# Expert results stored by route tile, rows gathered by token in the next stage: one core of a two-layer transformer kernel

## The reference, cut to what matters

```python
hn2 = _layernorm(x, ln2_g, ln2_b).reshape(-1, h)          # 4096 tokens
logits = hn2 @ gate_w + gate_b
idx = jnp.argmax(logits, axis=-1)                          # one of 8 experts per token
mid = jax.nn.relu(jnp.einsum('th,ehf->etf', hn2, w1) + b1[:, None, :])
y = jnp.einsum('etf,efh->eth', mid, w2) + b2[:, None, :]
moe = y[idx, jnp.arange(hn2.shape[0])]                     # only the chosen expert's row
return x + moe.reshape(b, s, h)
```

## Time and profile before

| what | us |
|---|---|
| median of the 3 runs shown | 1943.62 (1942.78 to 1947.55) |
| the profiled execution, its own time | 1934.06 |
| its span, first to last instruction | 1932.2 |
| mean granted PE clock over the span | 0.929 of full speed |
| PE busy / DVE / ACT / POOL in the span | 1711.6 / 1568.5 / 1332.0 / 1119.9 |

### The profile page before, as it was taken

One profiled execution on the slowest core, in us unless ns is written; L12 is line 12 of the kernel. 1 busy time (PEld: TensorE's weight loads), 2 busy tenths in 40 slices (PEclk: granted clock), 3 DMA queues, 4 the chain that ended last, 5 costly groups with the idle time before them and its releaser, 6 DMA issues. The chain is left out here.

```text
span 1932.2 us, 48344 instructions
## 1 busy us (share of the span) xinstructions
PE 1711.6 (89%) x18519; PEld 749.4 (39%) x18519; DVE 1568.5 (81%) x2890; ACT 1332.0 (69%) x2816; POOL 1119.9 (58%) x740
## 2 busy tenths in 40 slices
PE   6528756999999984969999999999999999999997
PEld 3328742233333354954432333333333333333334
DVE  7853466999999934648879999999999999999963
ACT  4502234688999852637866778887888888888885
POOL 8813553000010027431137889999999999989995
PEclk9769878799999975979988999999999999999998
DMA  1230027111111133248993332323232323233311
GB/s 49 33 56 4 2 75 272 36 45 47 45 45 47 33 108 108 74 116 292 405 365 87 82 81 76 87 69 87 70 89 68 89 71 86 75 81 80 77 29 44
DMA packets 194393, 178.08 MB, mean 92 GB/s; under 512 B 58740, under 2 KB 155156, under 8 KB 194084
## 3 DMA queue, kind: packets, MB, share of 16 engines
q1 hardware_dynamic: 185764, 167.93, 30.2%
q0 software_dynamic: 2944, 7.10, 1.2%
q10 hardware_dynamic: 5504, 0.73, 0.2%
HBM read 99.08 MB, written 75.26 MB: 90 GB/s over the span
## 5 line engine op out<-in xcount | busy, mean ns | idle before, releaser
L1038 ACT ACTIVATE probs_l<-exp_l 128x512 f32<-128x512 f32 x1024 | 575.6, 595 | 177.4 <-PE exp_l L1077 171.5
L976 DVE TENSOR_REDUCE maxima_l<-max_l 128x1 f32<-128x512 f32 x1024 | 640.5, 683 | 33.2 <-PE max_l L1122 33.1
L952 POOL TENSOR_TENSOR part_sums_l<-probs_l 128x1024 f32<-128x1024 f32 x256 | 604.0, 2359 | 91.5 <-ACT probs_l L1038 78.7
L1077 PE MATMUL exp_l<-q_stack_l,k_stack_l 100*128 100x512 f16 x1024 | 392.8, 385 | 3.4 <-ACT probs_l L1038 3.1
L1122 PE MATMUL max_l<-k_stack_l,q_stack_l 96*128 96x512 f16 x1024 | 387.2, 389 | 4.8 <-DVE pv_bank_l L968 3.6
L1361 DVE TENSOR_REDUCE maxima_l<-max_l 128x1 f32<-128x512 f32 x512 | 316.1, 683 | 13.3 <-PE max_l L1465 13.1
L1415 ACT ACTIVATE probs_l<-exp_l 128x512 f32<-128x512 f32 x512 | 278.8, 605 | 42.3 <-PE exp_l L1478 37.7
L1093 PE MATMUL pv_bank_l<-probs_l,v_ring_l 128*32 128x512 f32 x2048 | 273.7, 606 | 0.5 <-ACT probs_l L1038 0.5
L1077 PEld LDWEIGHTS exp_l<-q_stack_l,k_stack_l 100*128 100x128 f16 x1024 | 98.5, 97 | 395.0 <-ACT probs_l L1038 364.6
L1297 POOL TENSOR_SCALAR rstd_l<-squares_l 128x4 f32<-128x4 f32 x7 | 1.6, 234 | 339.9 <-ACT junk_l L1400 339.9
L958 POOL TENSOR_TENSOR part_sums_l<-part_sums_l 128x512 f32<-128x512 f32 x128 | 163.2, 1275 | 10.1
(11 more groups left out here) (305 smaller groups left out, 2422.6 us busy)
## 6 DMA issues: line engine op xcount, KB each, us to landing
scratch_qk_l<-parts_g SPq DMA_DIRECT2D x128, 256.0 KB, 9.2
q_stack_l<-scratch_qk_l SPq DMA_DIRECT2D x192, 128.0 KB
k_stack_l<-scratch_qk_l SPq DMA_DIRECT2D x192, 128.0 KB
scratch_v_l<-v_g SPq DMA_DIRECT2D x16, 1024.0 KB, 10.8
v_ring_l<-scratch_v_l SPq DMA_DIRECT2D x64, 256.0 KB, 3.4
scratch_stack_l<-parts_c SPq DMA_DIRECT2D x16, 384.0 KB, 3.5
q_stack_l<-scratch_stack_l SPq DMA_DIRECT2D x64, 96.0 KB, 2.2
k_stack_l<-scratch_stack_l SPq DMA_DIRECT2D x64, 96.0 KB, 2.3
```

What stands on the lines that cost most here:

```text
L952: pool.tensor_tensor(part_sums[:, i, h, :, :], probs[:, i, h, 0:2, :], probs[:, i, h, 2:4, :], ALU.add).then_inc(pair_sum.sem, 1)
L976: dve.reduce_max(maxima[:, s % 2, at % NT, at // NT:at // NT + 1], max_bank(n, at)[:, :], AX).then_inc(max_taken.sem, 1)
L1038: act.activation(probs[:, i, at // NT, at % NT, :], exp_ps[at % 2][:, :], ACT.Exp, scale=a.scale).then_inc(prob_tile.sem, 1)
L1077: pe.matmul(exp_ps[at % 2][:, :], ks[0:SHIFT_ROW + HG, slot, h, k * P:(k + 1) * P], qs[0:SHIFT_ROW + HG, slot, h, :], start=True, stop=Tru ...
```

## The change

The second scatter goes. Each route's result is stored by SP with a plain DMA to `by_route`, a DRAM tensor with one 128-row tile per route, ten routes behind the loads in SP's own stream. DVE works out for each token the row of `by_route` that holds its result (`g.dest`), behind the table. In the preparation POOL gathers each of the 32 tiles with an indirect DMA into `g.y`. The token number leaves the rows, so a row has 128 words.

```diff
-ROW = D + 1
-    r.rows, r.zeros = sb("rows", [P, T, ROW]), sb("zeros", [P, 2 * E_, ROW])
+    r.rows, r.zeros = sb("rows", [P, T, D]), sb("zeros", [P, 2 * E_, D])
-            did(pool.iota(r.rows[:, :, D:ROW]...))
-                did(pool.iota(r.zeros[:, :, D:ROW]...))
+STORE_LAG = 10
 # moe, SP
-            for i in range(ROUTES):
-                if i >= SLOTS:
-                    sp.wait_ge(y_out[i % DEPTH], 16 * ((i - SLOTS) // DEPTH + 1))
-                    sp.wait_ge(oneT_ps.sem, oneT_ps.made(i - SLOTS, 0))
-                at = sp.value_load(table[0:1, 0, i:i + 1], ...)
-                sp.dma_start(got[:, i % SLOTS, :], scratch.sorted[bass.ds(at, P), :]).then_inc(got_in[i % SLOTS], 16)
-            for s in range(DEPTH):
-                sp.wait_ge(y_out[s], 16 * (ROUTES // DEPTH))
-            for b in range(B):
-                sp.dma_start(g.y[:, b * NT:(b + 1) * NT, :], scratch.by_token[b * N:(b + 1) * N, :]...).then_inc(g.back_in[b], 16)
+            for i in range(ROUTES + STORE_LAG):
+                if i < ROUTES:
+                    if i >= SLOTS:
+                        sp.wait_ge(oneT_ps.sem, oneT_ps.made(i - SLOTS, 0))
+                    at = sp.value_load(table[0:1, 0, i:i + 1], ...)
+                    sp.dma_start(got[:, i % SLOTS, :], scratch.sorted[bass.ds(at, P), :]).then_inc(got_in[i % SLOTS], 16)
+                if i >= STORE_LAG:
+                    n = i - STORE_LAG
+                    sp.wait_ge(y_sb.sem, y_sb.made(n, 0))
+                    sp.dma_start(g.by_route[n * P:(n + 1) * P, :], y[:, n % DEPTH, :]).then_inc(y_out[n % DEPTH], 16)
 # moe, POOL
-            for i in range(ROUTES):
-                pool.wait_ge(y_sb.sem, y_sb.made(i, 0))
-                pool.wait_ge(got_in[i % SLOTS], 16 * (i // SLOTS + 1))
-                ids = got[:, i % SLOTS, D:ROW].bitcast(U32)
-                pool.indirect_dma_start(out=scratch.by_token[:, :], ..., in_=y[:, i % DEPTH, :]).then_inc(y_out[i % DEPTH], 16)
 # moe, DVE, behind dve.sem_inc(table_ready, 1); placed is now kept for all tiles
+                did(dve.tensor_tensor(to_route[:, :], ends[:, :], tiles[:, :], ALU.subtract))
+                did(dve.scalar_tensor_tensor(out=to_route[:, :], in0=to_route[:, :], scalar=float(P), in1=region[:, :],
+                                             op0=ALU.mult, op1=ALU.subtract))
+                did(dve.tensor_tensor(routed[:, :, :], choice[:, :, :], to_route[:, :].unsqueeze(1).broadcast_to([P, T, E_]), ALU.mult))
+                did(dve.tensor_reduce(by_route[:, :], routed[:, :, :], AX, ALU.add))
+                did(dve.tensor_tensor(g.dest[:, :], by_route[:, :], placed[:, :], ALU.add))
 # prep_l1, POOL
+            def gather(b, tiles):
+                for k in tiles:
+                    tile = b * NT + k
+                    pool.indirect_dma_start(out=g.y[:, tile, :], out_offset=None, in_=g.by_route[:, :],
+                                            in_offset=bass.IndirectOffsetOnAxis(g.dest[:, tile:tile + 1], 0)).then_inc(g.back_in[b], 16)
+            for s in range(DEPTH):
+                pool.wait_ge(g.y_out[s], 16 * (ROUTES // DEPTH))
+            gather(0, range(NT))
+            gather(1, range(NT // 2))
             power(0)
+            gather(1, range(NT // 2, NT))
             power(1)
+            gather(2, range(NT))
+            gather(3, range(NT))
             pool.wait_ge(beta_loaded, 16)
             for b in range(B):
                 ...
                 if b in MOMENTS_AT:
                     power(MOMENTS_AT[b])
+                if b < 2:
+                    for later in (2 * b + 4, 2 * b + 5):
+                        gather(later, range(NT))
 # prep_l1, DVE, moments_of_x
-                    dve.wait_ge(g.back_in[b], 16)
+                    dve.wait_ge(g.back_in[b], 16 * NT)
```

More of the change, by code:

```diff
@@ L1266, in _ @@
         def _(pool):
-            I32, r = mybir.dt.int32, g.router
+            r = g.router
             mine = [0]
@@ L1275, in settle @@
                 pool.wait_ge(pool_own, mine[0])
-            did(pool.iota(r.rows[:, :, D:ROW].bitcast(I32).rearrange("p k o -> p (k o)"), pattern=[[P, T]], base=0, channel_multiplier=1))
             did(pool.memset(r.zeros[:, :, :], 0.0))
@@ L1822, in moe @@
         table, tails = sb("table", [P, 2, ROUTES], I32), sb("tails", [P, E_], I32)
-        got = sb("got", [P, SLOTS, ROW])
+        got = sb("got", [P, SLOTS, D])
         oneT, w1_now = sb("oneT", [P, 2, P]), sb("w1_now", [P, 2, F_])
@@ L1836, in moe @@
         mid_sb, midT_sb, y_ps, y_sb = made("mid_sb"), made("midT_sb"), made("y_ps"), made("y_sb")
-        y_out = [sem(f"y_out{s}") for s in range(DEPTH)]
+        y_out = g.y_out
         w_qkv, w_qkv_loaded, w_scaled, w_first = sb("w_qkv", [P, QKV]), sem("w_qkv_loaded"), sem("w_scaled"), made("w_first", W_PIECES)
@@ L1958, in destine @@
                 settle()
-                did(dve.tensor_reduce(placed[:, :], place[:, :, :], AX, ALU.add))
+                did(dve.tensor_reduce(placed[:, at], place[:, :, :], AX, ALU.add))
                 settle()
-                dve.tensor_copy(dest[:, at], placed[:, :]).then_inc(dest_ready.sem, 1)
+                dve.tensor_copy(dest[:, at], placed[:, at]).then_inc(dest_ready.sem, 1)
             def tabulate():
@@ L2627, in program @@
         sem = phase_semaphores(nc, ctx, "_back")
-        g.back_in = [sem(f"back_in{b}") for b in range(B)]
+        g.back_in, g.y_out = [sem(f"back_in{b}") for b in range(B)], [sem(f"y_out{s}") for s in range(DEPTH)]
+        g.dest = ctx.enter_context(nc.sbuf_tensor("dest", [P, T], mybir.dt.uint32))
+        g.by_route = dram("by_route", (ROUTES * P, D))
         g.y = sb("y", [P, T, D])
```

17 lines of the change are left out of this document (8 added, 9 removed).

## The result

The changed kernel takes 1956.0 us (median of 11 runs, 1952.5 to 1960.0) against 1943.6 us for the kernel before, measured beside it: ratio 1.0064, 95% interval 1.0051 to 1.0077. It is slower by about 12 us where +0.8 was forecast, and the time lies above the range. The profiled execution took 1953.75 us, span 1951.9, to be read against 1934.06 and 1932.2 before.

What follows compares the result with a forecast made beforehand. PE was taken to bound the loop and, from about 900 us, the preparation, with a hole between them. -0.2 + 1.15 - 0.5 + 0.3 = +0.75 us on 1943.62 gave 1944.4 us, range 1938.5 to 1950.

Steps and rivals of the forecast that it cites:

- the loop: Expert loop: no change in time; period stays 1.89 us, POOL idle, a step of SP 1.65 to 2.0 us.
- the dispatch: Ahead of the loop: narrower rows may land sooner, -0.2 us, bounds 0 and -0.4.
- the place of DVE's idle stretch: Preparation, sign of being right: DVE idle 2 to 3 us ahead of the third group's second sum.
- signs of being wrong: Gathers over 1.7 us apart or landing after 3 us and more; PE waiting for loop loads; late stores idling PE.
- The hand-over, -1.8: Loop end to preparation: batch 0's gathers land at 850.5 against DVE's old start at 852.33, 1.8 us sooner.
- The third group, +1.15: Preparation, batches 2 and 3: late gathers end DVE's second sum 1.15 us later, passed to PE through the filter.
- The fourth and fifth, -0.5: Preparation, fourth and fifth groups: POOL's bias addition moves behind the gathers, easing DVE's shift; 0.5 us less PE waiting.
- DMA traffic, +0.3: Preparation: 1 MB of gathers adds some 1.3 us of backlog, mostly covered; +0.3 us, bounds 0 and +2.6.
- gathers held up by DVE: Preparation rival: each gather waits for a DVE operation, period 1.95 us; +8.4 us, 1952; chance 0.14.
- DMA-bound preparation: Preparation rival: the extra 1 MB isn't absorbed and moves the end by 2.6 us; +3.0, 1946.7; chance 0.12.
- Gathers in time: Preparation rival: gathers follow after 0.96 us, so the -1.8 lasts; -2.5 us, 1941.1; chance 0.14.
- SP at 2.4 us a step: Loop rival: SP's steps exceed 2.0 us, loads come late and the loop slows; +3 us at 2.4; chance 0.03.

Runs made afterwards that it cites:

- 4a, loads_in_prep: The kernel before with SP's eight loads of y moved to the head of the preparation: ratio 1.0021, hand-over 12.8 us.
- experiment 6: Three kernels: the changed one with gathers reordered (1.0057), gathers_sooner without the gathers of batches 4 to 7 (0.9993), the kernel before with 32 gathers for loads (1.0055).
- dest_padded: The changed kernel with the tensor dest declared at 256 instead of 128 bytes a partition: ratio 1.0059, preparation 166.6 us.
- gathers_sooner: dest_padded with POOL issuing the gathers of batches 1 and 2 one step sooner: ratio 1.0013, preparation 161.1 us.
- late-routing: Profiles, of 12 of 17 runs and the changed kernel's first, with slow routing ahead of the loop: first load 6.0 to 8.6 us behind the last scatter.
- after_again: The changed kernel, unaltered, profiled a second time: 1946.6 us where the median of the kernel before was 1932.1, preparation 169.7 us.
- before_filter_first: The kernel before with DVE taking the filter out of PSUM ahead of the third group's sum: ratio 0.9996, preparation 155.9 us.
- half_gathers: gathers_sooner without the gathers of batches 4 to 7, whose sums reuse the rows of batches 0 to 3: ratio 0.9993, preparation 156.3 us.
- before_gathers2: The kernel before, still scattering by token, with the eight loads replaced by 32 gathers in the order of gathers_sooner: ratio 1.0055, preparation 169.2 us.

## Why the prediction was wrong

**Right:** the loop (period, POOL idle, SP's step), the dispatch (in the second profile the first load is issued 2.9 us behind the last scatter, 3.3 before, for a forecast of -0.2), the spacing of gathers (1.26 us), the place of DVE's idle stretch ahead of the second sum of the third group (3.7 and 3.0 us for 2 to 3), and the path on which a delay of that group reaches PE. One of its own signs of being wrong came true: gathers that land after 3 us and more.

**The hand-over, -1.8, came out at +0.3 to +0.6.** The failed term is the landing: "2.2 us from issue to landing ... I take both" was 4.4 us, beside SP's constant loads; with them held back it was 2.6. The text had noted that these loads start sooner, and counted it only as a gain for ACT. It had also put the old hand-over down to SP's issues; experiments 4a and 6 show that the next part starts only some 7 us behind POOL's last scatter. The first gather came at 2.8 us for a forecast of 2.6.

**The third group, +1.15, came out at +4.0 to +4.7** (y's last operation to the filter: 32.3 before, 36.3 and 37.0 after). Of the 3.5 us that separate +4.7 from the forecast, 2.4 are the late landing of batch 0, which every later step inherits, 0.5 came in by the first of the eight gathers, and 0.5 with the one that took 1.46 us. Behind the long wait PE also works at the lower clock for 3 to 6 us. The 384 products of that form take 389 ns on average in dest_padded and 383 in gathers_sooner, which has neither the long wait nor a low clock behind it: 2.3 us in all. But the kernel before had 3.4 us at the lower clock behind its own wait, and its products take 388 ns, so against it the clock explains next to nothing. With the order mended wait and low clock both went, worth 5.5 us.

**The fourth and fifth, -0.5:** not seen. PE's waits for `parts` over the preparation were 6.3 us in five in the first profile and 3.4 in three in the second, before 3.4 in four.

**DMA traffic, +0.3, is the step that failed most.** It counted bytes at 405 GB/s and asked only whether they fit. First, the rate was not a constant of the sum: a declaration outside the loop moved every later buffer by 128 bytes, and 405 became 386 to 388. The lag grew by 5.1 and 6.6 us. No step looked at what a new persistent tensor displaces; on the kernel before it costs 5.4 us by itself. Second, beside the sixteen later gathers PE lost 4 to 5 us in late-routing profiles, and nothing in the others.

**The sum**, by the start of PE's products (us):

| stretch | before | after, first profile | after_again |
|---|---|---|---|
| y's last operation to the first product of batch 1 | 41.9 | 46.5 | 46.5 |
| batches 1 and 2 | 34.0 | 38.9 | 33.6 |
| batch 3 to the last product | 76.1 | 76.1 | 76.7 |
| last product to the last v store | 6.2 | 11.4 | 12.9 |
| the preparation | 158.2 | 172.8 | 169.7 |

The middle two rows of the kernel before, 34.0 and 76.1, are the same in the late-routing profiles of its edits (before_filter_first, loads_in_prep), so the first profile may be compared in them too.

So two losses are there in both profiles, 4.6 us by the hand-over and the third group and 5.1 to 6.6 by the shift, and one of 4.9 in the first alone. Without the shift, the late order and the sixteen gathers the preparation took 156.3 us (half_gathers), 1.9 under the kernel before; but 1.9 us is about what before's 3.4 us at the lower clock cost (1.7, my estimate from half the speed), and the runs (0.9993, 0.9980 to 1.0006) show no gain. That the change itself would gain is not shown.

The rival "gathers held up by DVE" had the nearest time (1952) and the wrong cause: they stayed 1.26 us apart. "DMA-bound preparation" had the right place, but its 2.6 us were for more bytes, where the rate fell. "Gathers in time" left its own +0.3 out of its sum (1941.4, not 1941.1), and SP at 2.4 us a step would lose 4.3 us past its lead, not 3; neither touches the forecast.

## What to carry to other kernels

Treat a new persistent buffer as a change to everything allocated behind it: pad it to 256 bytes, and test by adding an unused one to the old kernel. When a block load is replaced by many small transfers, count them on their issuing queue in order with all that stands behind, and place them where the DMA has room; here two edits tried one by one moved the runs' ratio by 0.0005 and 0.0007 and together by 0.0051, so try edits jointly before dropping either. Before subtracting two profiles, check that the parts which the change doesn't touch took the same time in both.

## What the runs showed of the hardware that was not expected

- 128 bytes of displacement in SBUF lower the rate of the full DMA with 2048-byte rows: between 953 and 969 us it is 383 to 389 GB/s in the six displaced kernels and 404 to 406 in the others, those displaced by 256 bytes among them.
- A part of the programme that follows POOL's indirect DMAs starts some 7 us behind the last of them (6.94 us of POOL's own idle time in before_gathers2; SP's loads at 858.99 behind a scatter that ended at 851.82 in loads_in_prep).
- A gather of 128 rows of 512 bytes was issued every 1.26 us beside a busy DVE too, with single ones that took 1.13 to 1.46 us themselves, instead of 0.95, where DVE's sum of two SBUF operands ran. In after_again a gather landed after 2.5 us at the least, 3.9 in the median and 7.2 at the most.
- Sixteen gathers beside stores cost PE 4 to 5 us in eight late-routing profiles and nothing in three others (experiment 6); the cause is open.
- The granted clock stood at 0.50 behind a PE wait of 5.9 to 6.7 us in the third group, and stayed at 1.00 behind one of 2.13 us in gathers_sooner, though in the first profile of the kernel before it fell to 0.52 behind a wait of the same 2.13 us.
